# A four-layer graph network on one core: the edge loops of layers 1 to 3 sum the current pair first and prepare later pairs further ahead

## The reference

```
w = relu(edge_feature @ W_fc1) @ W_fc2              # (E,64) @ (64,64) @ (64,224)
w0, w1, w2, w3, w4 = split(w, [64, 128, 160, 192])
xs, xv = s[dst], v[dst]                             # gathered node rows
out0a = w0 * xs
out0b = w3 * (einsum('emi,ei->em', xv, sh1) * INV_SQRT3)
out1a = (w1 * xs)[:, :, None] * sh1[:, None, :]
out1b = w2[:, :, None] * xv
out1c = w4[:, :, None] * (cross(xv, sh1[:, None, :]) * INV_SQRT2)
agg = segment_sum(concatenate([...]), src)          # (N, 480)
```

## Time and profile before

| loop | pairs | from the first product to the last, us | us per pair | granted clock |
|---|---|---|---|---|
| layer 1 | 440 | 1564 | 3.55 | 0.99 |
| layer 2 | 440 | 1614 | 3.67 | 0.96 |
| layer 3 | 440 | 1564 | 3.55 | 0.99 |

### The profile page before, as it was taken

How to read it: one execution, slowest core, us unless ns; L and a number is a source line. 1 busy time by engine, 2 the same in 40 slices (tenths; PEclk the granted TensorE clock), 3 DMA queues, 4 the chain that set the end, 5 groups by cost and what they waited for, 6 DMA issues and landing times. The chain is left out here.

```text
span 12096.9 us, 245491 instructions
## 1 busy us (share of the span) xinstructions
PE 9397.7 (78%) x46500; PEld 6592.8 (55%) x46501; DVE 9136.3 (76%) x32454; ACT 7003.3 (58%) x26255; POOL 6367.4 (53%) x9502
## 2 busy tenths in 40 slices
PE   4421188888888888888888788887788888788887
PEld 1211177777777777777777344445433335444445
DVE  6702078888888888888887899995565555899996
ACT  0000067777777777777776555553566666676764
POOL 0677646666666666666542455551355553455551
PEclk9855589999999999999998999996799999999997
DMA  6433211111111111111111343333222223343333
GB/s 262 53 66 70 64 31 31 30 30 30 30 31 30 31 30 30 31 30 31 27 17 38 82 87 86 87 85 46 43 53 52 52 52 54 84 87 85 86 85 60
DMA packets 1798441, 691.91 MB, mean 57 GB/s; under 512 B 1586190, under 2 KB 1677258, under 8 KB 1798346
## 3 DMA queue, kind: packets, MB, share of 16 engines
q0 software_dynamic: 219136, 411.56, 14.6%
q1 hardware_dynamic: 1572154, 275.26, 13.5%
q10 hardware_dynamic: 7056, 4.02, 0.1%
HBM read 514.24 MB, written 171.77 MB: 57 GB/s over the span
## 5 line engine op out<-in xcount | busy, mean ns | idle before, releaser
L963 POOL DMA_INDIRECT shared<-table,rec x2640 | 2560.4, 970 | 2508.8 <-issue 1058.4
L1045 PE MATMUL bank<-tp,oh 128*128 128x480 f32 (+1 forms) x5280 | 2407.3, 552 | 6.3 <-DVE tp L1122 4.6
L997 ACT ACTIVATE tp<-tp,rec 128x64 f32<-128x64 f32 x7920 | 2030.3, 335 | 234.1 <-DVE tp L1093 153.2
L1037 PE MATMUL bank<-w_fc,hT 128*128 128x448 f32 x2640 | 1368.5, 601 | 701.5 <-ACT hT L981 447.9
L1680 ACT ACTIVATE shared<-bank 128x512 f32<-128x512 f32 x1760 | 973.6, 595 | 961.9 <-PE bank L1755 955.1
L1045 PEld LDWEIGHTS bank<-tp,oh 128*128 128x128 f32 x5280 | 921.0, 195 | 856.8 <-issue 843.5
L1755 PE MATMUL bank<-ident,tp 128*128 128x128 f32 x7040 | 1054.0, 299 | 265.5 <-ACT tp L813 218.2
L1093 DVE TENSOR_TENSOR tp<-bank,shared 128x256 f32<-128x256 f32 x1320 | 560.2, 424 | 924.3 <-PE bank L1045 613.4
L782 POOL DMA_INDIRECT rec_dst<-ACC x784 | 813.5, 1038 | 602.5 <-issue 571.9
L1755 PEld LDWEIGHTS bank<-ident,tp 128*128 128x128 f32 x7040 | 889.9, 154 | 303.3 <-ACT tp L813 253.6
L1644 POOL DMA_INDIRECT gat<-table,rec x880 | 866.7, 985 | 277.0 <-issue 190.7
(11 more groups left out here) (248 smaller groups left out, 22541.0 us busy)
## 6 DMA issues: line engine op xcount, KB each, us to landing
shared<-table,rec POOLq DMA_INDIRECT x2640
rec_dst<-tp SPq DMA_DIRECT2D x44, 900.0 KB, 23.6
ACC<-in_attrs SPq DMA_DIRECT2D x56, 623.0 KB
rec_src<-tp SPq DMA_DIRECT2D x44, 730.0 KB, 19.9
efr<-rec_src SPq DMA_DIRECT2D x440, 64.0 KB
efr<-rec_dst SPq DMA_DIRECT2D x440, 64.0 KB
ACC<-in_attrs SPq DMA_DIRECT2D x196, 130.0 KB
rec<-rec_dst SPq DMA_DIRECT2D x1320, 10.0 KB
```

Source lines behind the costliest of these rows:

```text
L963: nc.gpsimd.indirect_dma_start(out=gatx[:, u, g, 0:L.row], out_offset=None, in_=tables[L.n][:, :], in_offset=IOff(ap=rec[:, u, g, L.idx:L. ...
L997: done = nc.scalar.activation(t[:, g, lo:lo + 64], t[:, g, 0:64], ACT.Copy, scale=rec[:, u, g, L.y + k:L.y + k + 1])
L1037: nc.tensor.matmul(pW[u % 2][:, 0:448], hT[:, u % 2, :], fc2[:, :], start=True, stop=True)\
L1045: done = nc.tensor.matmul(pS[u % 2][:, 0:TW], oh[:, u, g, :], tp[:, u % 2, g, 64:64 + TW], start=g == 0, stop=g == G - 1)
```

## The change

In the edge loops of layers 1 to 3:

- PE does both tiles of `sums(j)` first, then `weights(j+2)`, then `transposed(j+4)` (it was j+3), then `hidden(j+3)`.
- `pH` moves to a bank of its own (bank 6). `transposed(j)` now waits for `features(j-1)`, no longer for `activated(j-1)`; `hidden(j)` takes over that wait.
- ACT does `features(j+3)` (it was j+2), still followed by `activated(j+2)`.
- SP loads the record of pair j and then the features of pair j+2, with semaphores of their own (`rec_in`, `ef_in`). The load of the features waits for the transpose that frees their slot. POOL and DVE wait for the record alone. `scaled` has one wait more, for the record.

```diff
-            rec_in = [mark(f"rec_in{u}", 32 * QP) for u in range(4)]
+            rec_in = [mark(f"rec_in{u}", 16 * QP) for u in range(4)]
+            ef_in = [mark(f"ef_in{u}", 16 * QP) for u in range(4)]
...
-            pE, pH, ramp = BK[0][:, 0:128], BK[0][:, 128:256], BK[1][:, 0:P]
+            pE, pH, ramp = BK[0][:, 0:128], BK[6][:, 0:128], BK[1][:, 0:P]
...
-                    with sp.Fori(1, QP) as i:
+                    with sp.Fori(1, QP - 1) as i:
                         for u in range(4):
                             records(i, u)
+                            attributes(i + (u // 2), (u + 2) % 4)
...
                     def scaled(i, u):
+                        ac.wait_ge(rec_in[u].h, rec_in[u].at(i * 16 + 16))
                         ac.wait_ge(w_ready.h, w_ready.done(i, u))
...
+                        if not end or last(u, 3):
+                            features(*after(i, u, 3))
                         if not end or last(u, 2):
-                            features(*after(i, u, 2))
                             activated(*after(i, u, 2))
...
                     def transposed(i, u, first=False):
-                        pe.wait_ge(rec_in[u].h, rec_in[u].at(i * 32 + 32))
+                        pe.wait_ge(ef_in[u].h, ef_in[u].at(i * 16 + 16))
                         if not first:
 
+                            pe.wait_ge(ef_ready.h, ef_ready.free(i, u, 1))
...
                     def step(i, u, end=False):
+                        sums(i, u, 0)
+                        sums(i, u, 1)
                         if not end or last(u, 2):
                             weights(*after(i, u, 2))
-                        sums(i, u, 0)
-                        if not end or last(u, 3):
-                            transposed(*after(i, u, 3))
-                        sums(i, u, 1)
+                        if not end:
+                            transposed(i + 1, u)
                         if not end or last(u, 3):
                             hidden(*after(i, u, 3))
```

More of the change, by code:

```diff
@@ L942, in records, with attributes @@
                             sp.sem_inc(sp_tick, 1)
-                        load_records(sp, L, i, u, rec_in[u].h)
+                        lo, w = L.head
+                        sp.dma_start(rec[:, u, :, 0:w], L.records[i, u, :, :, lo:lo + w]).then_inc(rec_in[u].h, 16)
+                    def attributes(i, u, first=False):
+                        if not first:
+                            sp.wait_ge(ef_t.h, ef_t.free(i, u, 4))
+                            sp.sem_inc(sp_tick, 1)
+                        sp.dma_start(efr[:, u, 0:G * L.efw].rearrange("p (g f) -> p g f", g=G),
+                                     L.records[i, u, :, :, L.ef:L.ef + L.efw]).then_inc(ef_in[u].h, 16)
                     for u in range(4):
                         records(0, u, True)
-                    with sp.Fori(1, QP) as i:
+                        attributes(0, u, True)
+                    for u in range(2):
+                        attributes(1, u)
+                    with sp.Fori(1, QP - 1) as i:
                         for u in range(4):
                             records(i, u)
+                            attributes(i + (u // 2), (u + 2) % 4)
+                    for u in range(4):
+                        records(QP - 1, u)
+                        if u < 2:
+                            attributes(QP - 1, u + 2)
                 @block.gpsimd
@@ L956, in gather @@
                     def gather(i, u):
-                        po.wait_ge(rec_in[u].h, rec_in[u].at(i * 32 + 32))
+                        po.wait_ge(rec_in[u].h, rec_in[u].at(i * 16 + 16))
                         po.sem_inc(pool_tick, 1)
@@ L1011, in _ @@
                         activated(0, u)
+                    features(0, 2)
                     if L.y0 is not None:
@@ L1022, in transposed, with hidden @@
                     def transposed(i, u, first=False):
-                        pe.wait_ge(rec_in[u].h, rec_in[u].at(i * 32 + 32))
+                        pe.wait_ge(ef_in[u].h, ef_in[u].at(i * 16 + 16))
+                        if not first:
+                            pe.wait_ge(ef_ready.h, ef_ready.free(i, u, 1))
+                        nc.tensor.transpose(pE[0:EW, :], efr[:, u, 0:EW], ident[:, :]).then_inc(ef_t.h, 1)
+                    def hidden(i, u, first=False):
+                        pe.wait_ge(ef_ready.h, ef_ready.done(i, u))
                         if not first:
                             pe.wait_ge(hid_ready.h, hid_ready.free(i, u, 1))
-                        nc.tensor.transpose(pE[0:EW, :], efr[:, u, 0:EW], ident[:, :]).then_inc(ef_t.h, 1)
-                    def hidden(i, u):
-                        pe.wait_ge(ef_ready.h, ef_ready.done(i, u))
                         nc.tensor.matmul(pH, fc1[0:EW, :], efT[0:EW, u % 2, :], start=True, stop=True)\
@@ L1087, in along @@
                             return w[:, :, lo:lo + 32].unsqueeze(2).to_broadcast([P, G, 3, 32])
-                        ve.wait_ge(rec_in[u].h, rec_in[u].at(i * 32 + 32))
+                        ve.wait_ge(rec_in[u].h, rec_in[u].at(i * 16 + 16))
                         ve.wait_ge(gat_in[u].h, gat_in[u].at(i * 32 + 32))
```

5 lines of the change are left out of this document (3 added, 2 removed).

## The result

The changed kernel took 12390.66 us (median of 4 runs, 12389.93 to 12399.03), the kernel before 12161.10 us in the same job (4 runs, 12148.45 to 12169.12): ratio **1.0191** (1.0174 to 1.0209), 230 us slower where 423 us less were forecast. Its profiled execution took 12391.35 us with a span of 12389.3 us.

The account below looks back on a forecast made before the run. A ring through ACT was taken to bound layer 2, DVE to be close behind in layers 1 and 3. Gains of 75, 326 and 22 us, together 423, took 12166.5 to 11745 us; range 11570 to 11970.

Parts of the forecast that it names:

- The ring: Layer 2: PE's weights, sums, transpose and `hidden`, then ACT's activation, form a cycle of 3.27 us, which the change cuts.
- The regular distances: Undisturbed time from product to product after the change: 3.29, 2.64 and 3.40 us in layers 1, 2 and 3.
- Transfers: I cost this at nothing: Edge loops: the two moved loads per pair cost no time, since no product waits for either in regular pairs.
- Disturbances: a third or less goes: Means above regular distances by 0.15, 0.39, 0.15 us in layers 1 to 3 would shrink by 0.05, 0.10, 0.05.
- The sum: Gains of 75, 326 and 22 us in layers 1, 2 and 3, together 423 us.
- The falling clock: PE's idle gaps in layers 1 and 3 lower its clock, deciding from 0.87 down: slower, 12395 us; chance 0.04.
- POOL's rival: Layer 2 meets POOL's gather limit of 2.50 us first and ends at 3.2: gain 245 us, 11920 us; chance 0.19.

Follow-up runs that it names:

- after_fourth: The changed kernel unaltered, run again in a job of kind A: 11412.4 us, ratio 0.9763 to the kernel before.
- e5_before_paced: The kernel before, with each gather waiting for the product of three pairs earlier instead of four; kind A: 11692.5 us, ratio 1.0003.
- kind B: Jobs (sittings on one chip) in which the kernel before took 12076 to 12161 us; three jobs, the first measurement among them.
- e1b_transfers: The changed kernel's transfers and semaphores only, with the order of PE and ACT and the bank of before; kind B: 12287.3 us, ratio 1.0157.
- kind A: Jobs (sittings on one chip) in which the kernel before took 11691 to 11702 us; four jobs.
- e3b_paced: The changed kernel, with each gather waiting for the product of three pairs earlier instead of four; kind B: 12055.7 us, ratio 0.9968.
- e6: The change's transfers alone, with gathers waiting for the product of three pairs earlier instead of four; two runs, kind A: ratios 0.9996 and 0.9994.
- e8: The changed kernel with gathers held for the product of three pairs earlier and attributes' transfers issued by ACT; three runs, kind A: 0.9772, 0.9765, 0.9779.
- the paced form of the change: The changed kernel, with each gather waiting for the product of three pairs earlier instead of four: 0.9762 in kind A, 0.9968 in kind B.
- before_again: The kernel before, unaltered, run once more for a trace in a job of kind B: 12059.0 us.
- jobs 2 and 4: Two follow-up sittings: the first (kind B) reran both kernels unaltered, the second (kind A) ran four variants with held or delayed gathers.
- after_third: The changed kernel unaltered, run again beside three variants in a job of kind B: 12306.0 us, ratio 1.0174.

## Why the prediction was wrong, point by point

**The ring and its cut: right.** In after_fourth PE's weights (its row on the page) waited 3.1 us for the activation in the whole kernel:

```profile
L1061 PE MATMUL bank<-w_fc,hT 128*128 128x448 f32 x2640 | 1215.0, 542 | 3.1 <-ACT hT L999 3.1
```

**The regular distances: right in two layers, 5% short in the third.** Forecast 3.29, 2.64 and 3.40; after_fourth's means are 3.288, 2.816 and 3.394, its median in layer 2 is 2.76. The stretches of after_fourth:

```profile
6562.00:8006.00 1444.00, 185.12 (x440) 1.00 0.45 92
8314.00:9552.00 1238.00, 186.94 (x440) 1.00 0.41 67
9724.00:11215.00 1491.00, 185.97 (x440) 1.00 0.43 89
```

Its timeline in layer 2 shows the missing 0.13:

```profile
9002.34 0.21 DVE L1144 TENSOR_TENSOR tp<-t_sum,bank 128x64 f32<-128x64 f32 x1
...
9002.58 0.48 PE L1055 MATMUL bank<-efT,w_fc 32*128 32x128 f32 x2
...
9002.99 1.56 PE L1069 MATMUL bank<-tp,oh 128*128 128x385 f32 x4
...
9003.15 0.42 DVE L1118 TENSOR_TENSOR tp<-bank,shared 128x256 f32<-128x256 f32 x1 [0.60 <-ACT bank L1006]
...
9004.39 0.91 PE L1061 MATMUL bank<-w_fc,hT 128*128 128x448 f32 x2
9005.14 0.27 PE L1048 MATMUL bank<-ident,efr 128*32 128x128 f32 x1
9005.34 0.48 PE L1055 MATMUL bank<-efT,w_fc 32*128 32x128 f32 x2
9005.75 1.56 PE L1069 MATMUL bank<-tp,oh 128*128 128x385 f32 x4
...
9005.92 0.42 DVE L1118 TENSOR_TENSOR tp<-bank,shared 128x256 f32<-128x256 f32 x1 [0.60 <-ACT bank L1006]
```

The product ends at 9002.55 and the sums begin at 9002.99, 0.44 later, where I had 0.22: PE is not idle then but still in the transpose and `hidden` of the step before. PE has no wait in brackets anywhere here: it is full. In 1100 us of layer 2 it is busy for 1092 (columns as in the earlier trace rows):

```profile
8400.00:9500.00 1100.00, 1092.14 (x3552) 570.62 (x3550) 852.40 (x2761) 948.43 (x3943) 746.79 (x789) 1.00 0.40 68
```

789 gathers are 394 pairs (the forecast said 375), so PE's work per pair is 2.77 us, not the 2.37 that I added up from columns. From start to start the four groups take 1.40, 0.75, 0.20 and 0.41 (sums, weights, transpose, `hidden`), where I had 1.30, 0.75, 0.11 and 0.21. The rows that I had said so: 895 us for 302 pairs are 2.96 each, part of them at the lower clock (e5_before_paced has 951 us for 336 pairs, 2.83, at 1.00), and PE's only pause in a regular pair was 0.44 of 3.28.

**"Transfers: I cost this at nothing": the step that failed.** In kind B they cost 185 us by themselves (e1b_transfers), in kind A nothing. I looked only for products that wait for a gather, in a regular pair, and for waits of SP; that SP's own instructions were sometimes over 20 times as long (146 to 232 slow ones per loop in the trace that I had) I did not read, since no view counts them as busy. It was to be had from the longest value of SP's line, 892 ns for a register move where the median is 24. That no product waits for a gather was nearly right (0.6 us in 1100 of the transfers alone); what it left out are the spells, in which SP steps slowly and ScalarE takes its input late.

**"Disturbances: a third or less goes": failed, with the wrong sign.** Over the regular distances the means rise from 0.15, 0.39 and 0.15 to 0.53 (3.82 - 3.29), 1.07 (3.83 - 2.76) and 0.40 (3.80 - 3.40). I took them to belong to the kernel and its ring, the 2.42 us before `activated` among them, which hold such a late hand-over: in that trace `hidden` had ended at 9118.67, 1.65 us before `activated` began. The kernel before in kind A has 3.42, 3.30 and 3.42 (e5_before_paced, whose edit changes nothing, ratio 1.0003): nearly nothing is left of them in layer 2. They belonged to the job, and what the change does to them could not be had from the ring.

**The sum.** In kind A the change brings 0.131, 0.482 and 0.025 us per pair (against e5_before_paced), 58 + 212 + 11 = 281 us, which is the measured 11693.5 - 11412.4. Of the 423 forecast, layers 1 and 3 were 97 and came to 69, layer 2 was 326 and came to 212: of the 114 missing there, 44 are the 0.10 of disturbance that I let go of and that kind A does not have, and 70 the regular pair, 0.48 shorter and not 0.64. In kind B nothing of the 281 is left: transfers alone 1.0157, with the new order 1.0174.

**The rivals.** The falling clock gave 12395, and 12391 was measured. That is chance, since its mechanism is not what happened: the granted clock is 0.97, 0.91 and 0.98, over the 0.87 at which it decides, and the transfers alone are as slow with 0.97, 0.94 and 0.97. In after_fourth, without the spells, it is 1.00 in all three loops, so the lower clock goes with the pauses; what it costs in its turn was not separated. An estimate from the first rows above: (1 - clock) times the length, 50 + 152 + 33 = 235 us at the most, of the 860 by which the three loops are longer than after_fourth's. Gathers end 101.5 us of DVE's waits in layer 2, which was the sign for POOL's rival; there POOL itself had waited for records (223.2 us) and for products (135.2). A case in which the moved transfers cost more than the reordering brings was missing altogether.

**Left open.** Why the transfers alone double the slow instructions of SP, and ScalarE's late hand-overs, in layers 1 and 3. In their kernel a gather starts 7.05 us (median, layer 1) after the start of the product four pairs earlier, in the kernel before 7.72, in e3b_paced 7.52, and the share in the second gather is 21% against 8 and 6%: with the earlier start the second gather falls on SP's work for the next pair. That is argued from counts, and it rests on how they are made: if only the gather's own time is counted, without the 0.4 us behind it, the shares are 17%, 10% and 18%. The two runs that would have tried it (e6, and e8 for the amount of SP's work) all fell into jobs of kind A. What makes a job of kind B is open as well, and so is what an engine waits for in a spell: no view shows it.

## What to carry to other kernels

Before a transfer is given a cost of nothing, read the longest duration of the issuing engine's own instructions (SP's registers, waits), not only who waits for the data, and look for hand-overs between engines that are sometimes 50 times as long as the usual: such spells belong in the forecast, and in kind B earlier and longer rows of gathers went with more of them. Split the time of a loop into its regular distance and the rest, and ask whether the rest is the kernel's: the kernel before has to be seen in more than one job for that, since the same edit was worth 0.976 in one kind and 1.019 in the other. Where both kinds occur, the paced form of the change (one number) is the one to take: 0.9762 and 0.9968, faster than the kernel before in its one job of either kind.

## What the runs showed of the hardware

- The same kernel took 11691 to 11702 us in four jobs and 12076 to 12161 in three. The difference of the profiled kernels lies in the loops (4453 against 4693 us, e5_before_paced, whose edit changes nothing, and before_again) and outside them (7231 against 7364). The number of the chip doesn't decide it: jobs 2 and 4 both ran on number 13.
- In the longer kind SP's cheap instructions take about 0.7 us in spells, most of all beside gathers that POOL issues without a gap. Over the whole changed kernel 1659 of SP's 16888 are slow, 354 of POOL's 10719, 287 of DVE's 25803, and none of ACT's 9754.
- In the same spells ScalarE starts late on input that TensorE has finished: up to 5.5 us late, 138, 77 and 37 times over 0.5 us in the three loops of after_third, never over 0.04 us in after_fourth, the same kernel in a job of kind A.
- Issuing a plain DMA of 16 KB takes ScalarE's sequencer 0.56 us (e8_act, layer 2, 0.55 to 0.60).
